# Feed-forward attention outputs kept with features on partitions, gathered and divided by way of device memory

## The reference

```
x + attention(xn) + ffn(xn)
attention: 16 heads of 64, rotary, causal softmax, W_out
ffn:  q, k, v = xn @ Wq + bq, ...            16 heads of 8, no mask
      ctx  = softmax(q k^T / sqrt(8)) v
      y    = xn + layernorm(ctx @ Wo + bo) * g1 + be1
      gate = softmax(y @ Wg + bg), the two largest of 8 experts
      y + layernorm(sum of top value * (y @ We[e] + bexp[e])) * g2 + be2
```

## Time and profile before

| | us |
|---|---|
| median of 3 runs (lowest, highest) | 1212.21 (1206.92, 1213.35) |
| the profiled execution | 1212.86 |
| its span in the profile | 1211.0 |
| PE busy | 1086.8 (90%) |
| DVE busy | 858.8 (71%) |
| ACT busy | 828.8 (68%) |
| POOL busy | 816.2 (67%) |
| mean granted clock of PE | 0.963 |

### The profile page before, as it was taken

The page is one execution under the profiler, slowest core; times in us unless marked ns, Lnnn a source line. Parts: engine busy times, 40 slices in busy tenths (PEclk is TensorE's granted clock), DMA queues, the critical chain, the costliest instruction groups (busy, mean ns, idle before and its releaser), DMA issues.

```text
span 1211.0 us, 24662 instructions
## 1 busy us (share of the span) xinstructions
PE 1086.8 (90%) x8858; PEld 680.9 (56%) x8858; DVE 858.8 (71%) x2267; ACT 828.8 (68%) x1761; POOL 816.2 (67%) x753
## 2 busy tenths in 40 slices
PE   4688989999898998999988899998999999899996
PEld 3255656556574565756556455654656556565465
DVE  6666686766768568775879758786687776668557
ACT  4487766686657767588674877658776687566772
POOL 2675867587665688577775877649578568755780
PEclk9698999999889999999999999999999999699999
DMA  6112221122111132022211122112221122112111
GB/s 186 41 47 60 68 60 59 54 66 92 45 45 60 47 89 69 27 69 86 76 35 37 60 86 86 32 46 81 69 69 40 51 61 81 30 48 58 66 41 33
DMA packets 64741, 74.30 MB, mean 61 GB/s; under 512 B 22374, under 2 KB 34408, under 8 KB 64620
## 3 DMA queue, kind: packets, MB, share of 16 engines
q1 hardware_dynamic: 61148, 69.79, 18.6%
q10 hardware_dynamic: 3472, 2.95, 0.8%
HBM read 22.64 MB, written 3.67 MB: 22 GB/s over the span
## 4 chain that ended last, share of the span: by engine, by line
PE 63%; ACT 13%; DVE 12%; issue 4%; DMA 2%; POOL 2%; SPq 1%; ACTq 0%; POOLq 0%; DVEq 0%
PE work L1744 11%; PE work L1729 8%; PE work L1756 8%; PE work L1794 7%; DVE fnmax L1496 7%; PE work L1651 6%; ACT fpt L1334 5%; PE work L1653 5%; PE work L1652 5%; ACT pn L1389 4%; PE work L1766 4%; PE work L1775 4%; PE work L1784 3%; PE work L1655 1%; ACT raw L1359 1%
## 5 line engine op out<-in xcount | busy, mean ns | idle before, releaser
L1496 DVE TENSOR_REDUCE fnmax<-work 128x2 fp32r<-128x1024 f32 x256 | 302.3, 1218 | 82.4 <-PE work L1775 81.4
L1231 POOL TENSOR_TENSOR raw<-raw,cos_t 128x512 f32<-128x512 f32 x128 | 164.2, 1283 | 278.1 <-DMA swapped<-raw 275.7
L1389 ACT ACTIVATE pn<-work,nmax 128x512 f32<-128x512 f32 (+3 forms) x512 | 265.4, 537 | 73.8 <-DVE nmax L1609 69.8
L1609 DVE CUSTOM_DVE_ANT_0 work<-work,causal 128x512 f32<-128x512 f32 (+3 forms) x512 | 237.6, 517 | 107.9 <-PE work L1729 107.4
L1334 ACT ACTIVATE fpt<-work 128x1024 f32<-128x1024 f32 x256 | 251.0, 1028 | 76.3 <-PE work L1784 68.6
L1744 PE MATMUL work<-consts,pn 128*128 128x128 f32 x1280 | 182.1, 288 | 16.2 <-ACT fpt L1334 5.7
L1744 PEld LDWEIGHTS work<-consts,pn 128*128 128x128 f32 x1280 | 148.8, 147 | 61.3 <-DVE fnmax L1496 16.6
L1401 ACT COPY pt<-work 128x1024 f32<-128x1024 f32 x128 | 128.9, 1018 | 62.8 <-PE work L1744 62.6
L1235 POOL TENSOR_TENSOR raw<-raw,swapped 128x512 f32<-128x512 f32 x128 | 163.8, 1279 | 10.0
L1246 POOL TENSOR_TENSOR qk_l<-raw,qk_h 128x512 fp32r<-128x512 f32 x128 | 163.1, 1282 | 2.7
L1232 POOL TENSOR_TENSOR swapped<-swapped,sin_t 128x512 f32<-128x512 f32 x128 | 164.3, 1284 | 0.0
(11 more groups left out here) (153 smaller groups left out, 1790.4 us busy)
## 6 DMA issues: line engine op xcount, KB each, us to landing
swapped<-raw SPq DMA_DIRECT2D x256, 128.0 KB, 2.1
l_wide<-l_turned SPq DMA_DIRECT2D x128, 128.0 KB, 2.9
fqs<-fqn SPq DMA_DIRECT2D x96, 128.0 KB
x_in<-in_L_attn_x_dram SPq DMA_DIRECT2D x8, 256.0 KB, 3.9
out_dram<-x_in SPq DMA_DIRECT2D x7, 256.0 KB, 2.5
fpt<-in_L_attn_W_qkv_dram ACTq DMA_DIRECT2D x3, 512.0 KB, 6.4
l_turned<-l_inv SPq DMA_DIRECT2D x64, 16.0 KB
pt<-in_L_ffn_We_dram ACTq DMA_DIRECT2D x1, 512.0 KB, 9.6
```

The costliest lines, as they stand in the source:

```text
L1231: nc.gpsimd.tensor_tensor(raw[:, n % 3], raw[:, n % 3], cos_t[:], ALU.mult)
L1389: ins = nc.scalar.activation(pn[:, h, PN_AT[j]:PN_AT[j] + n], bank_of(("sc", b, c, unit), h)[:, at:at + n], ACT.Exp, scale=-1.0, bias=nmax ...
L1496: nc.vector.tensor_reduce(fnmax[:, g % 2, j * GH + 2 * r:j * GH + 2 * r + 2].unsqueeze(2), bank_of(("fsm", b, g, j), 2 * r, 2).rearrange(" ...
L1609: ins = nc.vector.tensor_tensor_reduce(out=scores, in0=scores, in1=causal[:, S - n:S], scale=-1.0 / math.sqrt(DH), scalar=3.0e38, op0=ALU.add,
```

## The change

The outputs are not turned. For each group SP writes the block of `fo` to device memory (`oput`, 128x512, 256 KB, a DMA). When the four groups of a batch have landed, `oget` reads back two 128x512 blocks: the 128 output rows into `ct`, and the 16 sums, each repeated on the 8 partitions of its head, into `ct_sums`. `fdiv` is now one step a batch: a reciprocal of 128x512 and a product of 128x512, both in SBUF. `ch` and `cl` read `ct` from SBUF. The steps `fT` and `cT` are gone, and with them their PSUM banks.

`ct` is no longer held by `cT` but by `cl`, and `fo`, a single buffer, by the landing of the DMA that reads it. All of `PLACE` and `PSUM` was written again by the planner (1130 steps on PE become 1090, 1028 on DVE 1004, 365 on SP 405; ACT and POOL keep 1038 and 430). The places of the new steps, in short: DVE has `fdiv` of batches 1 and 3 between `max(7, 2, 0)` and `max(7, 2, 1)`, the three numbers being pair, unit and half; of batches 0 and 4 in front of `max(7, 0, 0)`; of batch 5 in front of `max(6, 2, 0)`; of batches 2 and 6 behind `max(6, 2, 1)`; of batch 7 behind `max(6, 0, 0)`. ACT has `ch` of batches 1 and 3 in front of `exp(7, 2, 0)`, of batches 0 and 4 in front of `exp(7, 0, 0)`, of batch 5 behind `exp(7, 2, 0)`, of batch 2 behind `tpe(7, 0)`, of batch 6 behind `exp(6, 2, 1)`, of batch 7 in front of `exp(6, 0, 0)`. `wo` keeps its neighbours on PE in batches 0 to 6 (behind `fsm(1, 2)` of the next batch). In batch 7 PE has, behind the last `fpv`: `tq` of pair 5, `sc(5, 2)`, `pv` of pair 4, `tp(5, 0)`, `sc(6, 0)`, `tp(5, 1)`, `sc(6, 1)`, `sc(6, 2)`, `wo`.

```diff
@@ PLACE: new rows (the rest of PLACE and PSUM rewritten)
+    "oget": [
+        [47],
+        [98],
+        [143],
+        [196],
+        [251],
+        [299],
+        [349],
+        [396],
+    ],
...
@@ build
-        frec = sb("frec", [P, T, GH])
-        ct = sb("ct", [P, T, D])
+        ct = sb("ct", [P, S])
+        ct_sums = sb("ct_sums", [P, S])
...
+        o_rows = nc.dram_tensor("o_rows", [2, G, P, S], F32, kind="Internal").ap()
...
@@ SP
+                elif kind == "oput":
+                    g = x_[2]
+                    wait(sp, after("fo", b, g))
+                    wait(sp, landed("oget", b - 2))
+                    sp.dma_start(o_rows[b % 2, g], fo[:]).then_inc(oput_done[g % 2], 16)
+                elif kind == "oget":
+                    wait(sp, *(landed("oput", b, g) for g in range(G)))
+                    wait(sp, after("cl", b - 1))
+                    heads = o_rows[b % 2].rearrange("g (f r) n -> (g f) r n", r=STRIP)
+                    sp.dma_start(ct[:], heads[:, 0:FD]).then_inc(oget_done[b % 2], 16)
+                    sp.dma_start(ct_sums[:], heads[:, FD:FVW].broadcast_to([FH, FD, S])).then_inc(oget_done[b % 2], 16)
@@ ACT
                 elif kind == "fo":
                     g = x_[2]
                     wait(act, after("fpv", b, g, T - 1))
-                    wait(act, after("fT", *ring(1, b, g, G)))
+                    wait(act, landed("oput", *ring(1, b, g, G)))
                     nc.scalar.copy(fo[:], bank_of(("fpv", b, g, 0))).then_inc(done["fo"], 1)
                 elif kind == "ch":
-                    wait(act, after("cT", b))
+                    wait(act, after("fdiv", b))
                     wait(act, after("moe", b - 1, T - 1))
-                    nc.scalar.copy(ct_h[:], bank_of(("cT", b))).then_inc(done["ch"], 1)
+                    nc.scalar.copy(ct_h[:], ct[:]).then_inc(done["ch"], 1)
@@ DVE
                 elif kind == "fdiv":
-                    g = x_[2]
-                    sums = bank_of(("fT", b, g)).rearrange("p (t f c) -> p t f c", f=GH, c=STRIP)
-                    wait(dve, after("fT", b, g))
-                    nc.vector.reciprocal(frec[:].unsqueeze(3), sums[:, :, :, FD:FVW]).then_inc(dve_link, 1)
+                    wait(dve, landed("oget", b))
+                    nc.vector.reciprocal(ct_sums[:], ct_sums[:]).then_inc(dve_link, 1)
                     dve.wait_ge(dve_link, link())
-                    if g == 0:
-                        wait(dve, after("cT", b - 1))
-                    nc.vector.tensor_tensor(
-                        ct[:, :, g * GH * FD:(g + 1) * GH * FD].rearrange("p t (f d) -> p t f d", d=FD),
-                        sums[:, :, :, 0:FD], frec[:].unsqueeze(3).broadcast_to([P, T, GH, FD]), ALU.mult).then_inc(done["fdiv"], 1)
+                    nc.vector.tensor_tensor(ct[:], ct[:], ct_sums[:], ALU.mult).then_inc(done["fdiv"], 1)
                 elif kind in ("cl", "x2l"):
                     wait(dve, after("ch" if kind == "cl" else "x2h", b))
-                    nc.vector.tensor_tensor(ct_l[:], bank_of(("cT" if kind == "cl" else "x2T", b)), ct_h[:].bitcast(F32),
+                    nc.vector.tensor_tensor(ct_l[:], ct[:] if kind == "cl" else bank_of(("x2T", b)), ct_h[:].bitcast(F32),
@@ PE
-                elif kind == "fT":
-                    g = x_[2]
-                    wait(pe, after("fo", b, g))
-                    for t in range(T):
-                        ins = nc.tensor.transpose(psum[:, tile(t)], fo[:, tile(t)], ident)
-                    ins.then_inc(done["fT"], 1)
-                elif kind == "cT":
-                    wait(pe, after("fdiv", b, G - 1))
-                    for t in range(T):
-                        ins = nc.tensor.transpose(psum[:, tile(t)], ct[:, t], ident)
-                    ins.then_inc(done["cT"], 1)
```

More of the change, by code:

```diff
@@ L62 @@
         [0],
[L63 to L69, removed]
+        [78],
+        [208],
+        [343],
+        [479],
+        [616],
+        [753],
+        [887],
     ],
@@ L223 @@
+        [241, 307],
+        [377, 443],
+        [513, 579],
+        [649, 715],
+        [785, 851],
+        [921, 987],
+        [1056, 1089],
     ],
     "wo": [
-        [150],
-        [291],
-        [432],
-        [573],
-        [714],
-        [855],
-        [998],
-        [1109],
+        [145],
+        [282],
+        [417],
+        [553],
+        [689],
+        [825],
+        [963],
+        [1070],
     ],
     "x2T": [
-        [163],
-        [304],
-        [445],
-        [585],
@@ L450 @@
         [0],
-        [12],
-        [102],
-        [233],
-        [381],
-        [491],
-        [611],
-        [730],
+        [40],
+        [93],
+        [217],
+        [372],
+        [458],
+        [594],
+        [714],
+    ],
+    "wl": [
+        [5, 9, 20],
     ],
     "str": [
+        [1],
+    ],
+    "strl": [
         [2],
@@ L615 @@
+        [386],
+        [509],
+        [635],
+        [755],
+        [875],
+        [973],
     ],
     "ln1": [
[L617 to L624 removed]
+        [142],
+        [266],
+        [390],
+        [514],
+        [638],
+        [762],
+        [887],
+        [978],
     ],
     "x2l": [
[L627 to L633 removed]
@@ L634 @@
-        [1014],
+        [154],
+        [278],
+        [401],
+        [525],
+        [650],
+        [774],
+        [898],
+        [988],
     ],
     "gsub": [
-        [161],
-        [288],
-        [415],
-        [541],
-        [668],
-        [794],
-        [921],
-        [1017],
+        [158],
+        [282],
+        [405],
+        [530],
+        [653],
+        [777],
+        [901],
+        [992],
     ],
     "pick": [
-        [162],
-        [289],
-        [416],
-        [542],
@@ L896 @@
     "POOL": ("rs0", "rs1", "rs2", "rope", "hi", "lo", "x2", "res", "out"),
-    "SP": ("swap", "lput", "lget", "fdup", "mput", "mget", "store", "load"),
+    "SP": ("swap", "lput", "lget", "fdup", "mput", "mget", "oput", "oget", "store", "load"),
 }
@@ L907 @@
         KEYS[kind] = [(c, unit, h) for c in range(NC) for unit in range(3) for h in range(2)]
-    elif kind in ("fT", "fdiv", "fdup", "fo", "fturn", "mput", "mget"):
+    elif kind in ("fdup", "fo", "fturn", "mput", "mget", "oput"):
         KEYS[kind] = [(g,) for g in range(G)]
@@ L936 @@
 WIDE = {"tt": 2, "fqk": 2, "fsm": 4, "fst": 4, "moe": 2, "v": 2, "sc": 2, "tp": 2}
-FREED = {"tt": "tab", "tb": "qkb", "xT": "xl", "fv": "fvc", "fqk": "fqkl", "fsm": "fmax", "fst": "fexp", "fpv": "fo", "fT": "fdiv",
-         "cT": "cl", "wo": "nm1", "x2T": "x2l", "gate": "gsub", "moe": "moew", "proj": "raw", "v": "vc", "sc": "exp",
+FREED = {"tt": "tab", "tb": "qkb", "xT": "xl", "fv": "fvc", "fqk": "fqkl", "fsm": "fmax", "fst": "fexp", "fpv": "fo",
+         "wo": "nm1", "x2T": "x2l", "gate": "gsub", "moe": "moew", "proj": "raw", "v": "vc", "sc": "exp",
          "tp": "tpe", "tq": "tqe", "pv": "div", "ao": "yadd"}
@@ L1062, in build @@
         lget_done = [sem(f"lget{n}_done") for n in range(2)]
+        oput_done = [sem(f"oput{n}_done") for n in range(2)]
+        oget_done = [sem(f"oget{n}_done") for n in range(2)]
         mput_done = [sem(f"mput{n}_done") for n in range(2)]
@@ L1096, in landed @@
         def landed(kind, *key):
-            sems, per, dmas = {"fdup": (fdup_done, G, 4), "mput": (mput_done, G, 1), "mget": (mget_done, G, 1), "lput": (lput_done, NC, 1), "lget": (lget_done, NC, 2)}[kind]
-            n = key[0] * per + key[1]
+            sems, per, dmas = {"fdup": (fdup_done, G, 4), "mput": (mput_done, G, 1), "mget": (mget_done, G, 1), "oput": (oput_done, G, 1), "oget": (oget_done, 1, 2), "lput": (lput_done, NC, 1), "lget": (lget_done, NC, 2)}[kind]
+            n = key[0] * per + (key[1] if per > 1 else 0)
             return (sems[n % 2], 16 * dmas * (n // 2 + 1)) if n >= 0 else (begun, 1)
```

672 lines of the change are left out of this document (318 added, 354 removed), and 450 rows, old and new, of tables (PLACE, PSUM).

## The result

The changed kernel is slower: 1250.1 us in the median (1243.6 to 1256.1, 4 runs) against 1209.6 us of the kernel before beside it (1206.3 to 1213.4), a ratio of 1.033, interval 1.028 to 1.037. A second series gave 1.036 (1.031 to 1.040). The forecast was 1220 us with a range of 1197 to 1237. The direction was right, the size was not: some 41 us in place of 7.

What follows compares the result with a forecast made beforehand. PE was taken as the bound in long stretches, with DVE nearly as full in the short, deciding ones. Terms -18 - 3 + 18 + 5 + 2 + 3 = +7 on 1212.9 gave 1220 us, range 1197 to 1237.

Steps and rivals of the forecast that it cites:

- What bounds the kernel: PE bounds the long stretches; in the short ones around batch ends PE is busy 87% and DVE 84%, which decides.
- removed on PE: 128 `fT` and 32 `cT` transposes gone, 26.0 us busy, times PE's chain share 0.70: 18 us saved; lower bound nothing.
- the 3 us for DVE: 32 small reciprocals and products gone from DVE, 17.4 us, at its chain share of 0.17: 3 us saved.
- The reciprocal: In `fdiv` on DVE, 512 elements per partition at 6.0 ns each: 3.2 us, bounds 0.69 and 3.9 us.
- rival 3: Dearer reciprocal on DVE, 8.3 ns an element, 1.2 us more on each of eight, nothing hidden: +9, 1229 us; chance 0.1.
- What is queued behind `fdiv`: Batches 0 to 6: `fdiv` delays `max`, `ch` and `exp`, and so PE; 2.6 of 3.9 us count per batch: 18 us lost.
- The last batch: Batch 7, `fo` to `wo`: new chain 13.1 us against 7.8 us of PE work beside it, so PE idles 5 us.
- SP, DMA and `fo`: 48 more DMAs on SP mostly covered, but waits for `oput` hold SP and `fo`: 2 us lost, bounds nothing and 12.
- The new order: Steps planned again over the whole kernel: put at nothing, within 5 us either way.
- The clock: New PE gaps bring half-speed stretches: two counted at 1.5 us, 3 us lost, bounds nothing and 12.
- rival 2: ACT held at `ch`, 3.9 us reaching PE whole in seven batches, clock falling after each: +21, 1234 us; chance 0.15.
- The signs promised: Trace: reciprocals about 3.2 us, PE busy 26 us less, DVE 14 more, ACT idle before `ch`, 5 us gap before `wo`.

Runs made afterwards that it cites:

- The compact repair: Changed kernel with the reciprocal taken on compact 128x64 sums, then broadcast through device memory, and product, `ch` and `cl` in later places: 1.020 of the kernel before.

## Why the prediction was wrong

**What bounds the kernel.** Right as far as it went: the short stretches decide, and the whole loss lies in them and in batch 7. The use made of the chain was wrong. The step "removed on PE, 0.70 x 26.0 = 18 us" failed, and with it the 3 us for DVE. A share of the chain says how much of the old path ran over PE; it does not say what the next path costs once that work is gone. PE and DVE are both near the limit: 18 us are lost when 20 are added to PE, next to nothing is won when 26 are taken. The 26.0 us were too many to begin with: the busy times of single rows overlap their neighbours', and only 18.5 us of PE's busy time hang on the two lines. At equal clock the removal is worth some 5 to 9 us, and the clock takes these back. The term's lower bound, nothing, was the true value.

**The reciprocal.** 3.34 us against 3.2, and 1.13 against 0.69 for the product. The duration was sized well from 16, 8 and 4 elements; with 546 ns at 64, 942 at 128 and 3340 at 512, less the 157 ns of an instruction, it is 6.1 to 6.2 ns an element. That is six times the product's 1.04 ns. The eightfold that the repeat count in the Trainium skill (VectorE: DVE Perf Modes, the walkthrough of the 8-slice pipeline) would have given is not borne out, and rival 3 with it. The product and `cl` were taken over at 0.69 us with a bound of 0.1 us a batch; they took 0.44 and 0.38 us more, because GpSimd worked beside them (shown in the last section).

**What is queued behind `fdiv`.** Mechanism right, place for place: ACT held in front of `ch`, then `exp`, then PE's `fst`, `fsm` or projection. Only the size was off. I let 1.3 of 3.9 us be swallowed and counted 18 us; the gaps outside batch 7 are 22 us, and `fdiv` lasts 4.5 us. The reciprocals alone have a rest of 18 us (added to before) at equal clock. That ACT would not be held in front of `ch` in batch 2 was right (in batch 5 it wasn't either), but PE stood 3.96 us there all the same, since it waited for DVE itself; only batch 4 was covered.

**The last batch.** From `fo` to `wo` 13.1 us were forecast; the stretch to the end of `cl` took 13.6, and the gap in front of `wo` is 4.47 us where 5 were forecast. Right.

**SP, DMA and `fo`.** 2 us, and nothing in the runs speaks for more: DVE waits 0.2 us for its data, and in the new order the kernel with transfers and product but no reciprocal takes 1.003 of before, the one without all three 1.001. The new order was put at 0 within 5 us either way; it gives 1%, 12 us, with the new steps in it.

**The clock.** This is the step that failed by most: "I count two at 1.5 us: 3 us; bounds nothing and 12". By the yardstick about 28 us (22 to 31) are lost to it, some two thirds of the whole. The price of one stretch was taken as 3.5 us at most from a stretch of 7 us, though a stretch here lasts up to 17 us; and I counted two of them when seven gaps were to come. The range ended at 1237 because rival 2, which had the right mechanism ("the clock falls after each"), priced the clock at 6 us. With 28 in place of its 6, and without its 21 us for the removal but with the 5 to 9 that this gave, rival 2 would have come to 1268 to 1272 us, above the measured time, since it lets all of `fdiv` through; the forecast with those two terms put right comes to 1257 to 1261 us, 44 to 48 above its start of 1212.9. Measured are 1250, 41 above the kernel before beside it. The 28 are themselves taken from the measurement, so what this tests is the remainder: 16 to 20 us by the forecast's other terms, 14 measured.

**The signs promised.** The eight reciprocals, the missing transposes, DVE's growth (20 us for 14), ACT's idle time in front of `ch` and the gap in batch 7 came. PE's busy time "some 26 us less" did not: it rose by 16 us in this profile and by 4 in the later one, where 18.5 less were due, and that one line shows the missing term.

## What to carry to other kernels

Price a long hold of a nearly full engine by what it does to TensorE's clock afterwards, too: count the gaps that it will open on PE and take the length of the half-speed stretch behind such a gap from the trace, for every gap. A share of the chain of waits is no price. PE's share of 0.70 gives 14 us for the 20 added there, which cost 18; DVE's of 0.17 gives 5 us for 27 added, which cost 36; and for removed work it was an upper bound, since where two engines are both near the limit the gain can be nothing. Busy times of single rows of matmuls overlap; see what the engine's busy time is without them. Divide before you spread: a reciprocal's cost goes with the columns, so take it on the compact form of the sums.

## What the runs showed of the hardware

- Useless matmuls in the gaps made the kernel 14 us faster (1251 to 1238), by the split all of it through the granted clock (0.936 to 0.951). Where they left a gap of 3.4 us, 20.5 us at half speed followed.
- Reciprocal on fp32: 157 ns and 5.9 ns a column at 16 columns, 6.1 to 6.2 at 64, 128 and 512.
- Products of 128x512 with both sources in SBUF took between 0.69 and 1.7 us, those with one source in PSUM 0.69 us. In batch 3, where POOL was busy 0.34 of 4 us, it was 0.69; in batches 0, 1, 2, 6 and 7, with POOL at work beside them, 1.25 to 1.68. The Trainium skill (SBUF — State Buffer, SBUF: two separate sides) says that a VectorE operation with two SBUF inputs and a GpSimd operation that reads SBUF take a shared pair of ports in turn. The trace agrees, batch by batch. Where a GpSimd operation was already running, the product ended 0.55 us after that operation, in batches 0, 1, 2, 6 and 7 and in batch 5 too, where the operation had 0.18 us to go. Where both began together, as in batch 4, the product took 0.69 us and GpSimd's operation 1.83 in place of 1.28:

```profile
170.49 1.28 POOL L1247 TENSOR_TENSOR raw<-raw,swapped 128x512 f32<-128x512 f32 x1
170.86 1.45 DVE L1519 TENSOR_TENSOR ct<-ct,ct_sums 128x512 f32<-128x512 f32 x1
171.72 1.73 POOL L1258 TENSOR_TENSOR qk_l<-raw,qk_h 128x512 fp32r<-128x512 f32 x1
...
771.27 1.83 POOL L1247 TENSOR_TENSOR raw<-raw,swapped 128x512 f32<-128x512 f32 x1
771.27 0.69 DVE L1519 TENSOR_TENSOR ct<-ct,ct_sums 128x512 f32<-128x512 f32 x1
```

- Why the clock falls a little (0.968 to 0.955) when work is only removed is not settled. That PE then idles more does not suffice: with the transposes made twice PE had more work and idled 121 us for 124, and the clock was 0.958. The compact repair had 0.942 without a gap over 1.9 us before batch 7. The kernel before, too, runs some 90 us at half speed with no gap over 1.6 us behind the start-up; these stretches no experiment touches.
